# Second attention of a ViT tower: mixing products of two pairs of heads side by side, and four buffers of transposed probabilities

## The reference, cut to what matters

```python
qkv = x @ W_qkv                       # 192 -> 3 * 12 * 64, x is the layer norm of h
s = einsum('ghid,ghjd->ghij', q, k) * scale
a = softmax(s, axis=-1)
out = einsum('ghij,ghjd->ghid', a, v) # "mixing"
h = h + out @ W_0                     # 12 * 64 -> 192
```

## Time and profile before

| | |
|---|---|
| Median of three runs | 2720.94 us (2717.28 to 2723.74) |
| Profiled execution | 2716.97 us, span 2714.9 us |
| Second attention | 846 to 2462 us |
| TensorE busy, whole span | 2498.4 us (92%) |
| VectorE busy | 2254.3 us (83%) |
| ScalarE busy | 2089.7 us (77%) |
| GpSimd busy | 1232.4 us (45%) |
| Mean granted TensorE clock | 0.97 of full speed |

### The profile page before, as it was taken

How to read it: one execution, slowest core, us unless ns; L and a number is a source line. 1 busy time by engine, 2 the same in 40 slices (tenths; PEclk the granted TensorE clock), 3 DMA queues, 4 the chain that set the end, 5 groups by cost and what they waited for, 6 DMA issues and landing times. The chain is left out here.

```text
span 2714.9 us, 83446 instructions
## 1 busy us (share of the span) xinstructions
PE 2498.4 (92%) x27448; PEld 2120.4 (78%) x27448; DVE 2254.3 (83%) x5864; ACT 2089.7 (77%) x6198; POOL 1232.4 (45%) x1805
## 2 busy tenths in 40 slices
PE   5878886999997999999999999999999999996776
PEld 5767774888885888888888888888888888884554
DVE  6767876777775888888888888888888888887998
ACT  4867895555554888888888888888888888886998
POOL 6867882333331343434343334334433443344664
PEclk9988996999998999999999999999999999997999
DMA  6422330000001333333233333333333333320111
GB/s 202 134 81 84 103 90 1 1 0 0 0 0 37 73 81 68 74 72 80 67 73 75 79 68 70 77 77 70 67 80 74 73 67 80 72 63 14 40 43 46
DMA packets 181704, 173.54 MB, mean 64 GB/s; under 512 B 19063, under 2 KB 180289, under 8 KB 181378
## 3 DMA queue, kind: packets, MB, share of 16 engines
q1 hardware_dynamic: 181634, 172.64, 26.2%
HBM read 46.68 MB, written 9.68 MB: 21 GB/s over the span
## 5 line engine op out<-in xcount | busy, mean ns | idle before, releaser
L1323 POOL TENSOR_TENSOR b_pr<-b_pr,b_rinv 128x394 f32<-128x394 f32 (+1 forms) x768 | 626.5, 843 | 1006.8 <-DVE b_rinv L1281 1006.8
L1218 ACT ACTIVATE b_pr<-b_banks,b_nmx 128x197 f32<-128x197 f32 (+1 forms) x1536 | 625.8, 424 | 27.5 <-DVE b_nmx L1275 25.3
L1189 ACT ACTIVATE b_pt<-b_bank_t 128x394 f16<-128x394 f32 (+1 forms) x768 | 337.8, 494 | 202.7 <-PE b_bank_t L1154 202.5
L1275 DVE TENSOR_REDUCE b_nmx<-b_banks 128x2 f32<-128x394 f32 (+1 forms) x768 | 397.3, 558 | 65.5 <-PE b_banks L1144 57.3
L1246 DVE TENSOR_TENSOR b_pt<-b_bank_t,b_pt 128x394 f16<-128x394 f32 (+1 forms) x768 | 395.9, 556 | 18.2 <-ACT b_pt L1189 18.2
L1128 PE MATMUL b_banks<-b_xt,wqkv 128*128 128x197 f16 x3840 | 374.0, 249 | 4.4 <-DVE b_xt L1246 2.2
L1154 PE MATMUL b_bank_t<-ident,b_pr 128*128 128x128 f32 (+3 forms) x3072 | 341.8, 253 | 3.1 <-DVE b_pt L1246 3.0
L1128 PEld LDWEIGHTS b_banks<-b_xt,wqkv 128*128 128x128 f16 x3840 | 321.0, 98 | 25.5 <-issue 18.8
L1144 PE MATMUL b_banks<-b_kst,b_qst 128*128 128x197 f16 (+1 forms) x3072 | 326.7, 248 | 7.4 <-ACT b_pr L1218 4.9
L1154 PEld LDWEIGHTS b_bank_t<-ident,b_pr 128*128 128x128 f32 (+3 forms) x3072 | 282.1, 142 | 42.9 <-issue 35.4
L1218 ACT ACTIVATION_READ_ACCUMULATOR b_pr<-b_banks,b_nmx 128x1 f32 (+1 forms) x1536 | 315.0, 205 | 0.0
(11 more groups left out here) (206 smaller groups left out, 4665.0 us busy)
## 6 DMA issues: line engine op xcount, KB each, us to landing
b_qst<-b_qk SPq DMA_DIRECT2D x512, 147.8 KB, 2.5
b_kst<-b_qk SPq DMA_DIRECT2D x512, 73.9 KB, 2.3
patches<-in_x SPq DMA_DIRECT2D x64, 588.0 KB, 4.3
out<-z_res SPq DMA_DIRECT2D x32, 192.0 KB
out<-z_res SPq DMA_DIRECT2D x32, 103.5 KB
h<-in_wqkv SPq DMA_DIRECT2D x2, 1152.0 KB, 6.5
h<-in_w SPq DMA_DIRECT2D x2, 576.0 KB, 7.0
h<-in_fc SPq DMA_DIRECT2D x1, 768.0 KB
```

What stands on the lines that cost most here:

```text
L1189: return nc.scalar.activation(dst, src, ACT.Copy)
L1218: last = nc.scalar.activation(pr[n % 3][0:ROWS[c], c, e, :], banks[0:ROWS[c], c, e * SEQ:(e + 1) * SEQ], ACT.Exp, bias=nmx[n % 2][0:ROWS[c ...
L1275: v.reduce_max(nmx[n % 2][0:ROWS[c], c, :], banks[0:ROWS[c], c, 0:2 * SEQ].rearrange("p (e t) -> p e t", e=2), AX.X, negate=True).then_inc ...
L1323: last = nc.gpsimd.tensor_tensor(p, p, inv, ALU.mult)
```

## The change

The three orders are written anew, and the transposed probabilities get four buffers in place of two. In `PE_ORDER` the mixing blocks stand in three pairs (`m4^ m5^`, `m0 m1`, `m2 m3`), and the round is cut at another place. Scores, transposes and jobs have other neighbours: between s3 and s4 stand now q4' and t1 (before: m0, t1, q4'), between s5 and s0' now q5' and v1' (before: t2, q5', m1, v0', v1', t3). The lists of the other engines follow. The two new buffers lie in the first 1576 columns of `fc` and `fp`, the fp16 weights of the first MLP, which is over by then; the buffer of pair n is now `(2 * odd + n) % 4`, where `odd` is the image's parity, and ScalarE's copy waits for the mixing of four pairs back, not two. The number and form of all instructions of a round stay the same.

```diff
@@ -1004,14 +1004,14 @@
     h = S["h"]
     assert KEY_SCALE * QK_SCALE * QK_SCALE == float(DH) ** -0.5
     VH = 2 * D
-    PE_ORDER = ("x' v3 m3^ s1 t5^ m4^ q0' q1' s2 t0 m5^ q2' q3' s3 "
-                "m0 t1 q4' s4 w^ s5 t2 q5' m1 v0' v1' t3 s0' v2' "
-                "m2 t4 ").split()
-    ACT_ORDER = ("e0 t4^ x' v3 o1^ t5^ e1 q0' q1' t0 e2 q2' o2^ q3' "
-                "e3 q4' t1 e4 t2 q5' e5 v0' t3 o0 v1' v2' ").split()
-    DVE_ORDER = ("x' m1 v3 t5^ q0' q1' m2 r1 o1^ t0 r2 q2' m3 q3' "
-                "o2^ m4 n'' r3 q4' t1 m5 w^ q5' t2 r4 v0' t3 m0' "
-                "v1' v2' r5 r0' o0 t4 ").split()
+    PE_ORDER = ("q1' s2 t0 q2' m4^ m5^ q3' s3 q4' t1 s4 w^ v0' t2 "
+                "s5 q5' v1' s0' t3 m0 m1 v2' t4 x'' v3' s1' t5 m2 "
+                "m3 q0''").split()
+    ACT_ORDER = ("e0 v2 t4^ x' v3 t5^ e1 o0^ q0' q1' o1^ t0 e2 q2' "
+                "o2^ q3' e3 t1 q4' e4 v0' t2 e5 q5' v1' t3").split()
+    DVE_ORDER = ("q5 m0 t3^ r5^ v1 r0 v2 t4^ x' m1 v3 t5^ o0^ q0' "
+                "m2 r1 q1' t0 q2' r2 m3 q3' o1^ o2^ r3 n'' m4 q4' "
+                "t1 w^ v0' m5 r4 t2").split()
     JOBS = [s for s in PE_ORDER if s[0] in "xqvw"]
     assert len(JOBS) % 2 == 0
 
@@ -1053,6 +1053,8 @@
         val = [sb(f"b_val{r}", [P, 2, 2, HID], F16) for r in range(2)]
         pr = [sb(f"b_pr{r}", [P, 2, 2, SEQ]) for r in range(3)]
         pt = [sb(f"b_pt{r}", [P, 2, 2, 2 * SEQ], F16) for r in range(2)]
+        for used, form in (("fc", "p a b n -> p (a b n)"), ("fp", "p a f d -> p (a f d)")):
+            pt.append(S[used][:].rearrange(form)[:, 0:8 * SEQ].rearrange("p (a b t) -> p a b t", a=2, b=2))
         ot = sb("b_ot", [P, 2, PAIRS, SEQ], F16)
         nmx = [sb(f"b_nmx{r}", [P, 2, 2]) for r in range(2)]
         rsum = [sb(f"b_rsum{r}", [P, 2, 2]) for r in range(2)]
@@ -1167,7 +1169,7 @@
                                     head = 2 * n + e
                                     last = t.matmul(bank_o[e * DH:(e + 1) * DH, b, lo:lo + SEQ],
                                                     val[odd][0:ROWS[kc], pa, kc, head * DH:(head + 1) * DH],
-                                                    pt[n % 2][0:ROWS[kc], pb, kc, e * SEQ:(e + 1) * SEQ],
+                                                    pt[(2 * odd + n) % 4][0:ROWS[kc], pb, kc, e * SEQ:(e + 1) * SEQ],
                                                     start=(kc == 0 and j == 0), stop=(kc == 1 and j == 2))
                         last.then_inc(mixed, 1)
                     elif kind == "w":
@@ -1220,11 +1222,11 @@
                                                             accum_out=rsum[n % 2][0:ROWS[c], c, e:e + 1])
                             last.then_inc(freed[c], 1)
                     elif kind == "t":
-                        if later(PAIRS * img + n - 1):
-                            act.wait_ge(mixed, PAIRS * img + n - 1)
+                        if later(PAIRS * img + n - 3):
+                            act.wait_ge(mixed, PAIRS * img + n - 3)
                         for kc in range(2):
                             act.wait_ge(t_ready, 2 * (PAIRS * img + n) + kc + 1)
-                            copy(pt[n % 2][0:ROWS[kc], 0, kc, :], bank_t[0:ROWS[kc], kc, 0:2 * SEQ]).then_inc(pt_hi, 1)
+                            copy(pt[(2 * odd + n) % 4][0:ROWS[kc], 0, kc, :], bank_t[0:ROWS[kc], kc, 0:2 * SEQ]).then_inc(pt_hi, 1)
                     elif kind == "o":
                         act.wait_ge(mixed, PAIRS * img + 2 * n + 2)
                         if n == 0 and later(img):
@@ -1282,7 +1284,7 @@
                     elif kind == "t":
                         for kc in range(2):
                             dve.wait_ge(pt_hi, 2 * (PAIRS * img + n) + kc + 1)
-                            last = low(pt[n % 2][0:ROWS[kc], 1, kc, :], bank_t[0:ROWS[kc], kc, 0:2 * SEQ], pt[n % 2][0:ROWS[kc], 0, kc, :])
+                            last = low(pt[(2 * odd + n) % 4][0:ROWS[kc], 1, kc, :], bank_t[0:ROWS[kc], kc, 0:2 * SEQ], pt[(2 * odd + n) % 4][0:ROWS[kc], 0, kc, :])
                         last.then_inc(pt_split, 1)
                     elif kind == "o":
                         dve.wait_ge(ot_hi, 3 * img + n + 1)
```

## The result

The kernel after takes 2797.05 us (median of four runs, 2793.75 to 2797.68), the kernel before 2719.11 beside it: a ratio of 1.0283, 95% interval 1.0264 to 1.0302. It is 78 us slower; the forecast was no change (2720 us, with a range of 2696 to 2740). The profiled execution has a span of 2794.6 us.

The account below looks back on a forecast made before the run. TensorE, busy throughout, was taken to set the 24.77 us round. Own work of 23.79 plus three new waits of 0.38, 0.27 and 0.32 made 24.76 us, so 2720 us, range 2696 to 2740.

Parts of the forecast that it names:

- part 4: VectorE's queue from s3 to s0': margin 0.05 us, no cost taken, at most 0.3 us.
- rival B: VectorE's queue between r3 and m5 decides; at 0.25 us late a round, 2733 us; chance 0.21.
- Without waits: TensorE's own work in a round of the new order if nothing is late: 23.79 us, 0.98 less.
- rival C: TensorE drains between two adjacent mixing blocks as at a switch, 0.2 us a pair: 2748 us; chance 0.05.
- the toll of an island: Extra TensorE time for entering and leaving a separate group of mixing products: 0.22 us, three fewer a round.
- s4 behind s3: TensorE's second score block must wait for ScalarE to read the first one's scores: 0.38 us a round.
- s0' behind s5: The next image's first score block comes too early on TensorE and waits, 0.27 us with the refill.
- v3': TensorE's job waits for the bank of v2', whose copy stands behind t3's copies and an exponential: 0.32 us.
- w's cover over o2: VectorE's o2 ends 0.2 us before w begins thanks to wait 1; without that, w waits 0.2 us.
- wait 1: The wait of TensorE's s4 for the scores of s3 to be read: 0.38 us a round.
- That buffers, GpSimd's queue and the DMAs cost nothing: Added buffers lie in unread weights, GpSimd has over 1 us spare before every t, stacking DMAs have ten microseconds or more.
- Rival A: The new TensorE waits are shorter than forecast, likeliest that of v3', gaining 20 us: 2700 us; chance 0.22.

Follow-up runs that it names:

- e4: Kernel after, orders untouched, but GpSimd's product p3 held until the first half of VectorE's maximum m4 is done: 2722.39 us, 1.0021 of the kernel before.
- e1: Kernel after with one swap in VectorE's order, the normalisation n'' ahead of the reciprocal r3: 2721.1 us, 1.0013 of the kernel before.
- e8: Kernel of e5 with two of its three pairs of mixing blocks opened in TensorE's order, five islands for three: 2700.24 us, 0.9926 of the kernel before.
- e7: Kernel of e1 with the exponentials' row sums left out, so results are wrong and only time counts: 2680.86 us, 0.9866 of the kernel before.
- e3: Kernel before with only the four buffers of transposed probabilities and the later wait for the mixing, orders as before: 2716.76 us, 0.9996.
- e5: Kernel after, same pairs, buffers and instructions, with all three orders laid out anew by the traced latencies: 2670.62 us, 0.9827 of the kernel before.
- e2: Kernel before with the opposite swap, the reciprocal r3 ahead of the normalisation n'' in VectorE's order: 2782.57 us, 1.0235 of the kernel before.

## Why the prediction was wrong

**The step that failed is part 4, "VectorE from s3 to s0', no cost taken".** It lists "r3 (which waits for e3 ...), the normalisation 1.02 (1549.33 to 1550.35)" in this order, and takes the duration from a row in which GpSimd was idle (there n'' comes before the reciprocal). With p3 beside it, r3 and n'' take 2.42 us, not 1.11: 1.12 us of the difference are the clash with GpSimd, which the prediction put at nothing, and 0.19 the gap behind r3 (e4). It gave 0.3 as the upper bound of what VectorE could be late. The price of an instruction was carried over to a place where another engine was at work, without asking what that engine does there. The row itself could not show it; the order of r3 and n'' in the diff, read with the section of the Trainium skill named above, could.

The lateness of 1.31 us lands on TensorE where rival B said, and further up: v0' waits 0.69 for q4', t2 0.24 for t1's copy, s0' 0.54 where it would wait 0.31, together 1.16 us. That is the distance from 24.82 (e1) to 26.00 but for 0.02; by 62 rounds it is 73 us, the 73 that e1 measured. B had the right place and sign, and a size (0.25 us, 2733 us) five times too small. It did not have the cause: its queue was to be late by a margin added up too finely, not by instructions that take nearly three times as long.

**The rest held, nearly.** The order as predicted but without the clash is e4: its round is 24.89 us for a forecast 24.76, 0.13 more, and the kernel 1.0021 of the one before. With the normalisation ahead of r3 (e1) it is 24.82. Taking the terms one by one in e1, each from the starts of the blocks:

- Without waits: 24.82 less its waits of 1.05 is 23.77, forecast 23.79. A pair of mixing blocks has 0.08 between the blocks, the pace within a block, so rival C is out; the toll of an island is 0.21 as read and 0.23 as priced by e8.
- s4 behind s3: 0.39 for 0.38, of which 0.36 are between its halves. s0' behind s5: 0.31 for 0.27, and none with the shorter chain (e7).
- v3': 0.35 for 0.32. The size was right and the cause only partly: e7 took 0.37 us out of the chain that the prediction named and the wait stayed, held by the shorter path v2' to v3'. Here the size was right partly by luck.
- w's cover over o2 was real: when wait 1 went, w waited 0.10 to 0.14 for o2 (e7), for 0.2 forecast.
- That buffers, GpSimd's queue and the DMAs cost nothing: e3, and no row of TensorE waits for them.

Rival A, waits shorter than made, is refuted for the order that was predicted, and its thought was right for another: e5 keeps the pairs and has about 0.35 us of waits left in 24.13. There, 40 of the 61 us that the pairs could bring arrive in the steady rounds.

e5 is 46 to 49 us faster, while 0.64 us a round are 40. The rest lies in the start and end of the stage, which the prediction put at 0 with 3 us either way. In the traces the stage is 47.3 us shorter in e5: of this 38.9 are in the 61 rounds between the third x and the last (1510.8 us before, 1471.9 in e5), 4.2 ahead of them and 4.1 behind. Which waits those 8 us were, was not taken apart.

## What to carry to other kernels

When an instruction moves, its duration must be read again for its new neighbours: for a VectorE instruction from SBUF to SBUF such as these, ask what GpSimd does at that moment, and put it ahead of the semaphore that starts GpSimd's work, not behind. Where TensorE is busy throughout and VectorE and ScalarE for 88 and 83% of a round, as here, a gain on TensorE is kept only if the order is laid out against the fixed chains (here 2.9 us from one score block to the next): with the same pairs the kernel was 78 us slower in one order, about the same in a second (e1) and 46 us faster in a third (e5).

## What the runs showed of the hardware

- With GpSimd's fp32 product of 394 columns (0.84 us) beside it, a VectorE `tensor_scalar` of 128 fp32 columns from SBUF to SBUF took 0.86 to 0.92 us in place of 0.33, each until about 0.09 us after the product's end (the kernel after and e2). GpSimd's own duration did not change (median 0.84 in the kernels before and after, e1, e2, e4 and e5), and VectorE's maximum, which reads PSUM, kept its length beside p3 (1.01 us at 1503.48 in e1, for two).
- A change between products with 128 and with 64 columns of weights costs about 0.09 us on the way in (q takes 0.95 ahead of a mixing block, 0.86 elsewhere) and 0.10 on the way out, and 0.02 for the first pair, as read in the traces before and of e1. By e8 an island costs 0.23 us in all. Two mixing blocks directly behind each other pay none of this: 0.08 us from the last product of one to the first of the next (e1).
